# Two cross-attentions by query rows: norm, query projection, attention, output projection and next norm in one pass over chunks

## The reference

```python
# block 0: cross-attention behind an adaptive norm
x = x_q + softmax(q(adaln(x_q)) @ k(ctx)^T / sqrt(32)) @ v(ctx) @ Wp + bp
# block 1: self-attention, cross-attention, MLP
h = layer_norm(x) * (1 + scale_msa) + shift_msa
x = x + (mha(q, k, v of h) @ self_o_w + self_o_b) * gate_msa
h = layer_norm(x, norm2_g, norm2_b)
x = x + mha(h @ q_w + q_b, k, v of context @ kv_w + kv_b) @ cross_o_w + cross_o_b
h = layer_norm(x) * (1 + scale_mlp) + shift_mlp
x = x + (gelu(h @ mlp_w1 + mlp_b1) @ mlp_w2 + mlp_b2) * gate_mlp
```

## Time and profile before

| what | us |
|---|---|
| median of 3 runs | 4445.41 |
| the profiled execution | 4444.11 |
| its span, first to last instruction | 4442.3 |
| TensorE busy | 4022.1 |
| VectorE, ScalarE, GpSimd busy | 2441.3, 1845.4, 1606.0 |
| mean granted TensorE clock | 0.885 of 2.4 GHz |

### The profile page before, as it was taken

How to read it: one execution, slowest core, us unless ns; L and a number is a source line. 1 busy time by engine, 2 the same in 40 slices (tenths; PEclk the granted TensorE clock), 3 DMA queues, 4 the chain that set the end, 5 groups by cost and what they waited for, 6 DMA issues and landing times. The chain is left out here.

```text
span 4442.3 us, 61535 instructions
## 1 busy us (share of the span) xinstructions
PE 4022.1 (91%) x19596; PEld 2531.3 (57%) x19596; DVE 2441.3 (55%) x4225; ACT 1845.4 (42%) x3146; POOL 1606.0 (36%) x426
## 2 busy tenths in 40 slices
PE   4889969997999999999999999969799676999998
PEld 2655548883444444444444444447555454888887
DVE  2534454436777777777777777448444464232222
ACT  1434432222666666666666666634344333111111
POOL 0001120102777777777777777732011220000000
PEclk8865569996999999999999999989755687999999
DMA  6565545545021211202021211036555484111110
GB/s 199 142 152 137 137 145 188 185 148 112 22 63 25 50 38 33 54 19 59 22 63 25 63 24 27 20 115 210 138 137 137 135 291 142 39 47 67 38 38 28
DMA packets 234954, 412.39 MB, mean 93 GB/s; under 512 B 37793, under 2 KB 56433, under 8 KB 230621
## 3 DMA queue, kind: packets, MB, share of 16 engines
q1 hardware_dynamic: 234717, 409.40, 33.1%
HBM read 231.27 MB, written 152.90 MB: 86 GB/s over the span
## 5 line engine op out<-in xcount | busy, mean ns | idle before, releaser
L1062 ACT ACTIVATE a_e<-a_st 128x512 f32<-128x512 f32 (+1 forms) x2304 | 1224.5, 600 | 809.1 <-PE a_st L970 801.9
L1108 DVE TENSOR_REDUCE a_peak<-a_sm 128x1 f32<-128x512 f32 x2048 | 1274.5, 682 | 455.2 <-PE a_sm L948 441.1
L1180 POOL TENSOR_TENSOR a_esum<-a_esum,a_e 128x2048 f32<-128x2048 f32 x256 | 1172.1, 4578 | 126.4 <-ACT a_e L1062 113.7
L948 PE MATMUL a_sm<-a_k,a_q 96*128 96x512 f32 (+1 forms) x3072 | 1061.9, 401 | 80.5 <-DMA a_k<-s_k 59.0
L970 PE MATMUL a_st<-a_q,a_k 128*128 128x512 f32 (+1 forms) x2304 | 1043.3, 456 | 40.8 <-DMA a_q<-a_rows 32.4
L970 PEld LDWEIGHTS a_st<-a_q,a_k 128*128 128x128 f32 (+1 forms) x2304 | 446.1, 194 | 670.0 <-issue 298.3
L948 PEld LDWEIGHTS a_sm<-a_k,a_q 96*128 96x128 f32 x3072 | 670.3, 240 | 202.8 <-issue 60.6
L983 PE MATMUL a_acc<-a_e,a_v 128*32 128x512 f32 (+1 forms) x4608 | 668.6, 655 | 19.2 <-ACT a_sums L1076 16.6
L484 PE MATMUL p_po<-p_w,p_os 128*128 128x512 f32 x768 | 262.4, 425 | 108.9 <-DVE p_x L641 27.6
L1285 PE MATMUL mlp_ph<-mlp_us,mlp_w_hi 128*128 128x512 f32 x1024 | 336.1, 390 | 25.3 <-DVE raw_mlp_lo L1330 25.3
L1186 POOL TENSOR_TENSOR a_o<-a_sums,a_inv_t 128x512 f32<-128x512 f32 x96 | 122.4, 1275 | 591.2 <-DVE a_inv_t L1144 581.1
(11 more groups left out here) (108 smaller groups left out, 3878.4 us busy)
## 6 DMA issues: line engine op xcount, KB each, us to landing
a_q<-s_q SPq DMA_DIRECT2D x288, 256.0 KB, 5.0
s_q<-p_out SPq DMA_DIRECT2D x96, 512.0 KB, 4.6
a_q<-a_rows SPq DMA_DIRECT2D x96, 256.0 KB, 3.2
s_o<-a_o SPq DMA_DIRECT2D x96, 256.0 KB, 5.2
p_o<-s_o SPq DMA_DIRECT2D x24, 1024.0 KB, 6.8
s_x<-p_x SPq DMA_DIRECT2D x24, 1024.0 KB, 4.5
a_k<-s_k SPq DMA_DIRECT2D x24, 1024.0 KB, 15.6
p_x<-in_x SPq DMA_DIRECT2D x16, 1024.0 KB, 7.6
```

The costliest lines, as they stand in the source:

```text
L948: mm = pe.matmul(sm[:, bank_of_unit(j, u), x * KE:(x + 1) * KE], q[0:3 * DH, j % QR, h, qt * P:(qt + 1) * P], k[0:3 * DH, g % 2, h, kc * K ...
L1062: act.activation(e[0:KR, (j * NKT + kt) % ER, h], st[0:KR, place(kt, h) % RING], ACT.Exp, scale=SCALE).then_inc(score_read, 1)
L1108: dve.tensor_reduce(dst, src, AX.X, ALU.max).then_inc(unit_read, 1)
L1180: pool.tensor_tensor(esum[:], e[:, slot(0)] if x == 1 else esum[:], e[:, slot(x)], ALU.add).then_inc(e_added, 1)
```

## The change

p1, a1 and the first half of p2 become one `cross_pass` (stage name p1); so do p3, a3 and p4 (stage name p3). `dense_pass` (p2) is left of the old p2: it reads `u` from DRAM and makes q, k and v. There are six stages now.

A `cross_pass` runs through slots m = -1 to 8, and in slot m three chunks are in work: the attention of chunk m, the norm and the query projection of a = m + 1, and the output projection and the next norm of c = m - 1. p3 has in addition `own_rows`, the projection of the self-attention's output for chunk a, with the gate multiplied into the weights (`gate_weights`). Scores are made once, with queries on the partitions, in units of 4 heads x 128 rows (4 matmuls, two PSUM banks in turn). VectorE takes the maximum of a unit and subtracts it in PSUM (`unit_max`, `unit_sub`), ScalarE takes the exponential, VectorE sums it and inverts the sum (`inverse_sums`), GpSimd multiplies it in (`shares`), TensorE transposes the weights (`turn_weights`, 16 transposes of a group), ScalarE copies them (`take_weights`), and TensorE weighs (`weigh`). The Sqrt table is gone: the inverse root is exp(-0.5 ln v) on ScalarE (`inverse_root`) with one Newton step of four small operations on VectorE (`refine`). GpSimd now normalises (`normalise`), adds the bias row (`add_row`, `add_own_row`) and takes all rests of the activations (`rest`, `own_rest`). The q of a chunk still goes to DRAM and comes back. The MLP weights are loaded in `mlp` itself, by column pieces; its last 6 pieces are split on GpSimd beside the matmuls. The two passes are written out without loops.

```diff
@@ chunk_pass goes; cross_pass comes in its place @@
-def chunk_pass(nc, d, name, x_in, x_out, o_in, b_out, gate, eps, scale, shift, projections, values, raw, plain=None,
-               prefetch=None):
...
+def cross_pass(nc, d, name, x_in, x_out, own, k_in, v_in, q_mid, norm_q, norm_u, q_bias, b_out, u_out, raw, preload):
...
+    XR = 3
...
+        @block.sync
+        def _(sp):
...
+            def store_x(n):
+                b, i = place(n)
+                sp.wait_ge(pp_read, ring_number("out", n, TT - 1) + 1)
+                sp.dma_start(x_out[b, i * W:(i + 1) * W, :].rearrange("(t p) c -> p t c", p=P), x[:, n % XR]).then_inc(x_stored[n % XR], DMA)
+            def slot(m):
+                a, c = m + 1, m - 1
+                if has(m):
+                    load_q(m, 2)
+                if has(c):
+                    store_x(c)
+                if own is not None and has(m + 2):
+                    load_own(m + 2)
+                if has(m):
+                    load_q(m, 3)
+                if own is not None and m + 2 == CHUNKS:
+                    sp.dma_start(raw.raw[:, 0], channels(own_weight)).then_inc(w_again, DMA)
+                if has(a):
+                    store_q(a, 0)
+                    store_q(a, 1)
+                    load_q(a, 0)
+                if has(m + 2) and m + 2 >= XR:
+                    load_x(m + 2)
+                if has(c):
+                    store_u(c, 0)
+                    store_u(c, 1)
+                if has(a):
+                    store_q(a, 2)
+                    load_q(a, 1)
...
+        @block.tensor
+        def _(pe):
...
+            def scores(n, g):
...
+                pe.wait_ge(q_loaded[g % 2], 3 * DMA * ((n * G + g) // 2 + 1))
+                for qt in range(TT):
+                    unit = n * UNITS + g * TT + qt
+                    if unit >= 2:
+                        pe.wait_ge(exp_done, unit - 1)
+                    for h in range(GH):
+                        mm = pe.matmul(sm[:, unit % 2, h * KE:(h + 1) * KE], qs[0:3 * DH, g % 2, h, qt * P:(qt + 1) * P],
+                                       ks[0:3 * DH, b, g * GH + h], start=True, stop=True)
+                    mm.then_inc(sm_done, 1)
+            def slot(m):
+                a, c = m + 1, m - 1
+                if has(m):
+                    scores(m, 0)
+                if has(a) and own is not None:
+                    own_rows(a, (0, 1, 2, 3))
+                if has(c):
+                    out_rows(c, (0,))
+                if has(m):
+                    scores(m, 1)
+                if has(c):
+                    out_rows(c, (1, 2))
+                if has(m):
+                    turn_weights(m, 0)
+                if has(c):
+                    out_rows(c, (3,))
+                if has(m):
+                    scores(m, 2)
+                if has(a):
+                    turn(1, a, 0)
+                if has(m):
+                    weigh(m, 0)
+                if has(a):
+                    turn(1, a, 1)
+                if has(m):
+                    turn_weights(m, 1)
+                if has(a):
+                    turn(1, a, 2)
+                if has(m):
+                    scores(m, 3)
+                if has(a):
+                    turn(1, a, 3)
+                if has(m):
+                    weigh(m, 1)
+                if has(a):
+                    query(a, 0)
+                if has(m):
+                    turn_weights(m, 2)
+                if has(c):
+                    turn(2, c, 0)
+                if has(a):
+                    query(a, 1)
+                if has(c):
+                    turn(2, c, 1)
+                if has(m):
+                    weigh(m, 2)
+                if has(a):
+                    query(a, 2)
+                if has(c):
+                    turn(2, c, 2)
+                if has(m):
+                    turn_weights(m, 3)
+                if has(a):
+                    query(a, 3)
+                if has(c):
+                    turn(2, c, 3)
+                if has(m):
+                    weigh(m, 3)
...
+        @block.scalar
+        def _(act):
...
+            def slot(m):
+                a, c = m + 1, m - 1
+                if has(a) and own is None:
+                    inverse_root(1, a)
+                if has(m):
+                    exponentials(m, 0)
+                if has(a) and own is not None:
+                    inverse_root(1, a)
+                if has(m):
+                    exponentials(m, 1)
+                    take_weights(m, 0)
+                if own is not None and has(m + 2):
+                    own_split(m + 2)
+                if has(m):
+                    exponentials(m, 2)
+                if has(c):
+                    inverse_root(2, c)
+                if has(a):
+                    modulate(1, a, 0)
...
+        @block.vector
+        def _(dve):
...
+            def unit_sub(n, g, qt):
+                unit = n * UNITS + g * TT + qt
+                dve.wait_ge(top_done, unit + 1)
+                src = sm[:, unit % 2, 0:GH * KE].rearrange("p (h k) -> p h k", k=KE)[:, :, 0:S]
+                dve.tensor_tensor(src, src, top[:, unit % 4].unsqueeze(2).to_broadcast([P, GH, S]), ALU.subtract).then_inc(sub_done, 1)
+            def maxima(n, g):
+                for pair in ((0, 1), (2, 3)):
+                    for qt in pair:
+                        unit_max(n, g, qt)
+                    for qt in pair:
+                        unit_sub(n, g, qt)
+            def slot(m):
+                a, c = m + 1, m - 1
+                if has(m):
+                    maxima(m, 0)
+                if has(a) and own is not None:
+                    for tt in range(TT):
+                        add_rows("own", a, (tt,), own_biased)
+                    statistics(1, a, range(TT))
+                    spread(1, a)
+                if has(c):
+                    add_rows("out", c, (0,), biased)
+                    statistics(2, c, (0,))
+                if has(a):
+                    refine(1, a)
+                if has(m):
+                    inverse_sums(m, 0)
+                    maxima(m, 1)
+                if has(c):
+                    add_rows("out", c, (1, 2), biased)
+                    statistics(2, c, (1, 2))
+                if has(m):
+                    inverse_sums(m, 1)
+                if has(c):
+                    add_rows("out", c, (3,), biased)
+                    statistics(2, c, (3,))
+                    spread(2, c)
+                if has(m):
+                    maxima(m, 2)
+                    out_rest(m, 0)
+                if has(c):
+                    refine(2, c)
+                if has(m):
+                    inverse_sums(m, 2)
+                    maxima(m, 3)
+                    inverse_sums(m, 3)
+                    out_rest(m, 1)
+                if own is not None and m + 2 == CHUNKS:
+                    gate_weights(1)
+                if has(a):
+                    query_rest(a, 0)
+                    query_rest(a, 1)
+                if has(m):
+                    out_rest(m, 2)
+                if has(a):
+                    query_rest(a, 2)
+                    query_rest(a, 3)
+                if has(m):
+                    out_rest(m, 3)
+                if own is not None and m + 2 == CHUNKS:
+                    weights_rest(0, NW + 1)
+                if own is None and has(m + 2):
+                    statistics(1, m + 2, range(TT))
+                    spread(1, m + 2)
...
+        @block.gpsimd
+        def _(pool):
...
+            def shares(n, g):
...
+                for qt in range(TT):
+                    pool.tensor_tensor(e[:, number % 2, qt, :, 0:S], e[:, number % 2, qt, :, 0:S],
+                                       inv[:, number % 2, qt].unsqueeze(2).to_broadcast([P, GH, S]), ALU.mult).then_inc(norm_done, 1)
+            def slot(m):
+                a, c = m + 1, m - 1
+                if own is None and has(a):
+                    normalise(1, a)
+                if has(m):
+                    shares(m, 0)
+                if own is None and has(a):
+                    add_row(a)
+                if has(m):
+                    shares(m, 1)
+                if own is not None and has(a):
+                    normalise(1, a)
+                    add_row(a)
+                if has(a):
+                    rest(1, a, 0)
+                    rest(1, a, 1)
+                if has(m):
+                    shares(m, 2)
+                if has(a):
+                    rest(1, a, 2)
+                    rest(1, a, 3)
+                if has(c):
+                    normalise(2, c)
+                if has(m):
+                    shares(m, 3)
+                if own is not None and has(m + 2):
+                    own_rest(m + 2)
+                if has(c):
+                    for t in range(KT):
+                        rest(2, c, t)
+                if own is not None and has(m + 2):
```

(24 more changed lines are left out.)

938 lines of the change are left out of this document (542 added, 396 removed).

## The result

The changed kernel takes **4599.6 us** (median of 4 runs, 4594.7 to 4603.4) against 4445.0 for the kernel before: 1.0346 times as long, 95% interval 1.0333 to 1.0359. The forecast was 4495, with 4280 to 4690 around it. The sign held and so did the range, but the loss is 155 us where 50 were forecast, so some 105 us have to be found. The page of the profiled execution, its engines, its clock, and two of its groups (busy us, mean ns, idle before them).

A forecast was written before the change was run, and what follows sets the result against it. TensorE at half clock in the small attentions was the room; waits in the fused slots decided. To 4442.3 us of span came +40 (first pass and p2), +1 (second pass), +10 (MLP), and 1.8 around the span: 4495 us, range 4280 to 4690.

The forecast's parts named there:

- The frame: Small attentions at half clock, fused passes walked slot by slot: first pass 677 us with slots of 80, p2 280.
- The two waits for ScalarE behind VectorE's order: First-pass slot: TensorE stands about 5 us for exponentials, twice, because VectorE comes late to the maxima.
- the cast of 8192 columns took 7.0 us, so 0.6 us for 512 and one input: GpSimd's normalisation, not in the trace as such, priced at 0.6 us per 512 columns from a cast.
- The load behind the store of x: Second-pass slot: attention-output load issued at 39 us, landing about 7 later; TensorE stands from 40.5 to 49.
- The clock in the second pass: Second-pass slot: 86 us at full clock, 93 with the clock's losses.
- The ring of three: Second pass: ring of u has three tiles instead of four; the prediction had no term for a wait on it.
- The untouched stage: Self-attention, code unchanged: forecast at 1914.3 us, with no term for a change.
- The MLP: MLP: +10 us in all, some 4 for a later start and 6 for GpSimd's splits holding up VectorE.
- The signs: Passes: PEclk 0.65 to 0.85, slots 76 to 85 and 88 to 98 us, ScalarE idle 7 to 10, p2 280.
- The queries' round trip: Queries through DRAM: taken as hidden, 5 us each way in 13 us of other work; a wait would show the prediction wrong.
- The clock did rise: Answers the rival that the clock never rises in the passes: slots near 100 and 118, about 4830 us, chance 0.13.
- The rival on the other side, shorter waits: Both passes: clock hardly falls and load returns in time, slots 70 and 78, about 4305 us, chance 0.27.

The follow-up runs named there:

- 5: Kernel 3 with VectorE taking the maxima of group 1 ahead of the first output tile's work, and first-pass statistics earlier: 4442.2 us.
- 2: Changed kernel with both normalisations moved from GpSimd to VectorE: 4554.0 us.
- 4: Changed kernel with GpSimd's four normalisation operations each in another form, the normalisation left out of the result: 4568.8 us, run once.
- 3: Changed kernel with the attention-output load issued ahead of the store of x and both normalisations on VectorE: 4499.2 us.
- 9: Changed kernel with unread dense matmuls, 12 and 10 per slot, in TensorE's waits ahead of the third score units of groups 0 and 1: 4558.6 us.
- 6: Kernel 3 with the store of the first tile of u issued ahead of the load of the queries on SyncE's queue: 4482.0 us.
- 8: Kernel 7 with 37 repeated waits ahead of the self-attention's loop in TensorE's program: 4412.1 us, run once.
- 13: Kernel 7 with 8 repeated waits ahead of the self-attention's loop in TensorE's program: 4412.5 us, run once.
- 14: Kernel 7 with 20 repeated waits ahead of the self-attention's loop in TensorE's program: 4410.5 us, run once.
- 7: Kernel 3 with both VectorE's new order (5) and the early store of u (6): 4421.1 us, 0.9954 of the kernel before.

## Where the prediction held and where it failed

- **The frame held.** TensorE at 0.5 in the small attentions, 0.75 to 0.78 in the fused passes, walked slots of 80 against 78.5: the first pass came out 1.3% off, p2 1.5%. In part that is luck: in the first pass six slots were 11 us shorter than forecast, and its start, slot 0 and its end 19 us longer. The two waits for ScalarE behind VectorE's order, 5 us each walked, were 5.3 and 4.6, and turning that order round (5) took away 6.6 us a slot.
- **The step that failed: "the cast of 8192 columns took 7.0 us, so 0.6 us for 512 and one input".** I took the price of one GpSimd operation from the row of another, because both have one input. It is 2.09 us, so 8.3 a chunk where 2.4 were priced, twice a slot. The bound from the other side stood in the same rows: GpSimd's two-input operation, 1.28 us, which itself would have been too low. Moved to VectorE, it gives back 45.6 us (2), and cheaper forms in its old place give back 31 (4). With the load's wait gone it is worth more, 74 us (4572.8 to 4499.2). Of the 79.6 us that the second pass missed, the way to its first maximum has 15.6, and 6.3 of them went with this move.
- **The load behind the store of x** was seen and called the second pass's own wait. It was sized 8.5 us and was 11.2; the mistake was to let nothing lie beneath it.
- **The clock in the second pass** is the other term that was mis-sized: 7 us a slot, measured 15 to 17. The five full slots missed by 41 us in all, while in four of them TensorE was idle for 1.5 to 2 us less than the 30.8 walked (28.8 to 29.3; in the one with the gating, 35.3). 4 to 5 us a slot went with the stand for the load (3). The matmuls of 9 did not take the rest away: that pass fell by 13.4 us in all.
- **The ring of three** was in the code and not in the walk: 3.3 us at each slot's end, 17 us in all (6).
- **The untouched stage** was charged nothing and cost 13.7 us, by the place of its loop in TensorE's program (8, 13, 14). No row of the kernel before shows that a shift of the code could do this.
- **The MLP**: the term for GpSimd beside VectorE, 6 us, was 1; the late start, 4 us, was 12.6, because ScalarE waits for the small vectors first.
- **The signs.** PEclk (0.75 and 0.76), the first pass's slots and p2 came out as said; the second pass's slots (99 to 107 where 88 to 98 were said) and ScalarE's idle time before the split (11.5 where 7 to 10 were said) did not. The queries' round trip was hidden but for 7.6 us of TensorE's idle time over both passes. Two sums have small slips: 87.6 to 1005.4 is 917.8 us, not 917.4, and the four parts of the prologue add up to 44.6, not 46.
- **The rivals.** The clock did rise, though TensorE had mostly transposes and small matmuls: in the small work of a slot of the first pass it was granted 0.50 in the first 7 us behind the wait and 0.86 in the next 8.5 (stretch, length, TensorE busy, PEclk, DMA share, GB/s):

```profile
394.60:401.30 6.70, 5.86 (x26) 0.50 0.68 172
401.30:409.80 8.50, 6.76 (x48) 0.86 0.00 0
```

  By the rule of the Trainium skill, "TensorE: Matmul & The Clock Gate", Part 4, that transposes do not count as work, that stretch would have stayed at 0.5; with 24 transposes, 16 score matmuls and the 8 matmuls of a weighing it did not, and no run here has transposes alone. The Trainium skill's 769 ns for 512 elements on GpSimd ("GPSIMD Engine Reference", section 3.1) lies 0.16 above the copy's 0.61 and far below the 1.49 to 2.09 of the forms with scalars.
- The rival on the other side, shorter waits, asked for slots under 75 us. With the orders of 7 the slots are 71.6 and 82, near its 70 and 78, and the kernel is faster than before; but at 4421 us it is still 116 above the 4305 that this rival gave.

## What to carry to other kernels

Price an operation on GpSimd by a row of the same operation and operands, or leave its bounds wide: here a copy, a two-input operation and one with two scalars took 0.61, 1.27 and 2.09 us for the same tile. Where two engines' waits end at about the same time, removing one shows only the difference; remove both before you judge either. A fused loop is as good as the order on its helper engines: the same work, with a load, a store, a normalisation and one group of maxima issued elsewhere, went from 3.5% slower to 0.5% faster and to 0.8% with the self-attention's loop at a better place.

## What the runs showed that I had not expected

- Behind a long hardware loop's jump back to its start TensorE stood for 6.2 to 7.9 us with nothing to wait for, or for 1.3 to 2.3, depending on how many instructions stand ahead of the loop in its program: 8 added waits saved 13.8 us. The long stands end with a second 16 KB transfer of instructions.
- GpSimd's tile operation with scalars costs more (1.49 to 2.09 us) than its two-input one (1.27).
- GpSimd's splits of the attention output took 10.55 us for four beside VectorE's splits of the weights at the start of the second pass, 5.0 later in the same pass; what the earlier trace rows showed for VectorE happens in the other direction too. It is part of the 15 us by which that start was longer than walked.
